# Scores of the first three head pairs as three fp32r products each, in a macaron transformer block on one core

## The reference, cut to what matters

```python
x = x + 0.5 * ffn(layernorm(x))        # gelu(h @ w1 + b1) @ w2 + b2, hidden 1024
q, k, v = heads(layernorm(x) @ w_qkv)  # 16 heads of 64
sim = (q * 64 ** -0.5) @ k.T + slope[h] * -abs(i - j)
attn = softmax(where(j > i, -max, sim))
x = x + (attn @ v) @ w_out + b_out
x = x + 0.5 * ffn(layernorm(x))
```

## Time and profile before

| what | value |
|---|---|
| median of 3 runs (lowest, highest) | 2183.58 us (2183.23, 2184.14) |
| the profiled execution's own time | 2183.17 us |
| its span, first to last instruction | 2181.4 us |
| mean granted TensorE clock | 0.995 |
| busy: PE, PEld | 98%, 80% of the span |
| busy: DVE, ACT, POOL | 69%, 57%, 48% |

### The profile page before, as it was taken

One profiled execution on the slowest core, in us unless ns is written; L12 is line 12 of the kernel. 1 busy time (PEld: TensorE's weight loads), 2 busy tenths in 40 slices (PEclk: granted clock), 3 DMA queues, 4 the chain that ended last, 5 costly groups with the idle time before them and its releaser, 6 DMA issues.

```text
span 2181.4 us, 41803 instructions
## 1 busy us (share of the span) xinstructions
PE 2137.8 (98%) x14720; PEld 1738.8 (80%) x14720; DVE 1507.9 (69%) x4014; ACT 1237.4 (57%) x3096; POOL 1056.4 (48%) x1770
## 2 busy tenths in 40 slices
PE   7999999999999999999999999999999999999997
PEld 6688787877878788787887878878787787878876
DVE  6866767667676676776768676676766767667674
ACT  5745646466464664736557364574646646466472
POOL 1744627446273553726537174372744627355371
PEclk9999999999999999999999999999999999999999
DMA  3422505234051331514315052250523405134151
GB/s 131 131 74 73 141 1 159 56 88 126 15 151 49 108 107 34 152 28 118 96 56 137 22 140 74 70 143 2 156 58 91 123 15 151 49 108 107 35 137 43
DMA packets 109985, 193.91 MB, mean 89 GB/s; under 512 B 34512, under 2 KB 53200, under 8 KB 109776
## 3 DMA queue, kind: packets, MB, share of 16 engines
q1 hardware_dynamic: 88816, 137.95, 22.3%
q0 software_dynamic: 20480, 52.47, 9.7%
q10 hardware_dynamic: 480, 0.82, 0.1%
HBM read 14.95 MB, written 8.39 MB: 11 GB/s over the span
## 4 chain that ended last, share of the span: by engine, by line
PE 87%; ACT 4%; POOL 4%; DVE 3%; issue 1%; SPq 1%; DMA 1%; DVEq 0%; ACTq 0%; POOLq 0%
PE ps L302 85%; POOL P L983 3%; ACT P L629 2%; PE ps L356 2%; ACT L629 1%; DVE P L821 1%; SPq L245 1%; ACT qk L589 0%; DVE x L768 0%; DMA PT<-P 0%; DVE gl L739 0%; DMA raw<-in_L_ffn_w 0%; POOL PT L245 0%; DVE gh L788 0%; ACT gt L607 0%
## 5 line engine op out<-in xcount | busy, mean ns | idle before, releaser
L983 POOL TENSOR_SCALAR P<-P,rs 128x512 f32<-128x512 f32 (+3 forms) x1024 | 540.7, 546 | 441.8 <-DVE rs L804 438.4
L629 ACT ACTIVATE P<-P,mx 128x512 f32<-128x512 f32 (+3 forms) x1024 | 564.1, 555 | 194.8 <-DVE mx L813 194.6
L245 POOL DMA_DIRECT2D PT<-P x640 | 322.7, 510 | 238.1 <-DVE P L821 216.3
L821 DVE STREAM_TRANSPOSE P<-P 128x1792 f32<-128x1792 f32 (+1 forms) x256 | 374.2, 1486 | 13.2 <-POOL P L983 12.7
L302 PE MATMUL ps<-PT,v 128*64 128x256 f32 (+1 forms) x3072 | 306.9, 349 | 8.5 <-DMA PT<-P 8.5
L302 PE MATMUL ps<-qk 64*128 64x512 f32 (+3 forms) x2048 | 311.0, 443 | 0.7 <-ACT qk L589 0.7
L302 PE MATMUL ps<-w2h,gh 128*128 128x256 f32 x1024 | 292.8, 286 | 0.6 <-DVE gl L739 0.4
L302 PE MATMUL ps<-w2l,gh 128*128 128x256 f32 x1024 | 289.7, 283 | 0.0
L302 PE MATMUL ps<-w2h,gl 128*128 128x256 f32 x1024 | 289.5, 283 | 0.0
L302 PEld LDWEIGHTS ps<-PT,v 128*64 128x64 f32 x3072 | 205.5, 137 | 104.6 <-issue 15.7
L589 ACT ACTIVATE qk<-ps 128x512 f32<-128x512 f32 x256 | 153.2, 598 | 228.0 <-PE ps L302 227.9
(11 more groups left out here) (83 smaller groups left out, 4403.7 us busy)
## 6 DMA issues: line engine op xcount, KB each, us to landing
PT<-P SPq DMA_DIRECT2D x1398, 80.0 KB, 2.6
PT<-P POOLq DMA_DIRECT2D x640, 80.0 KB, 2.7
x<-in_L_attn_x SPq DMA_DIRECT2D x16, 512.0 KB, 4.2
out_y<-x SPq DMA_DIRECT2D x15, 512.0 KB, 3.2
raw<-in_L_ffn_w SPq DMA_DIRECT2D x2, 512.0 KB, 5.8
raw<-in_L_ffn_w SPq DMA_DIRECT2D x1, 1024.0 KB, 8.8
rawq<-in_L_attn_w_qkv SPq DMA_DIRECT2D x1, 1024.0 KB, 6.8
rawk<-in_L_attn_w_qkv SPq DMA_DIRECT2D x1, 1024.0 KB, 8.8
```

The source lines that it names most:

```text
L245: e.dma_start(PT[c % 2][32 * m:32 * m + 32, g, :], P[c % 3][32 * g:32 * g + 32, m, :]).then_inc(landed.sem, 16)
L629: e.activation(p, p, ACT.Exp, bias=mx[:, r, i:i + 1], scale=-1.0, accum_out=sm[:, r, i:i + 1]).then_inc(s_ex.sem, 1)
L821: e.transpose(p, p).then_inc(s_tr.sem, 1)
L983: e.tensor_scalar(p, p, rs[:, 2 * (c % 2) + h, i:i + 1], 1.0, ALU.mult, ALU.mult).then_inc(s_nz.sem, 1)
```

## The change

It touches `scores` on TensorE, `proj_copy` on ACT, DVE's order, one wait of POOL, and the q and k buffers.

- Pairs c < NS = 3 of each batch (heads 0 to 5) are scored as three fp32r products: high with high, high with low, low with high, for each i, the two heads alternating inside each product. Pairs 3 to 7 stay in float32.
- For those pairs ACT, right behind the float32 copy of q, copies q and k together (128 x 1024) into `qkh` as fp32r, and DVE writes the low part over the float32 tile (`qkl` has the place of `qkf`). `scores` waits for that. ACT's copy waits for its own copy of q.
- DVE does this `qk_lo` for pair 1 behind the eight `gelu_split` and ahead of `add3(b - 1, 0)`; for pair 2 behind `add3(b - 1, 2)` and ahead of `inverse(b, 1, 1)`; for pair 0 of the next batch behind `normal(3, b, ...)` and ahead of `ln_lo(3, b, 0)`. POOL's `bias(3, b)` waits for the last of these.
- `add3(b - 1, 1)` moves ahead of the first half of `turned(b, 0)`.
- k is now stored in the order in which the scores read it, and `proj_copy` waits for the scores of the pair directly before; TensorE issues those scores ahead of the projection anyway.

```diff
+    NS = 3
+    qkh = place("qkh", [128, 2, T], F32R, QK)
+    qkf_at = [PP + 10240] + [QK + 4096] * (NS - 1) + [QK + 4096 * (c % 2) for c in range(NS, NC)]
+    qkf = [place(f"qkf{c}", [128, 2, T], F32, a) for c, a in enumerate(qkf_at)]
+    qkl = [place(f"qkl{c}", [128, 2, T], F32R, a) for c, a in enumerate(qkf_at[:NS])]
...
             def scores(b, c):
-                e.wait_ge(s_pc.sem, s_pc.at((b, ("q", c))))
+                if c < NS:
+                    e.wait_ge(s_kl.sem, s_kl.at((b, c)))
+                    parts = ((qkh, qkh), (qkh, qkl[c]), (qkl[c], qkh))
+                else:
+                    e.wait_ge(s_pc.sem, s_pc.at((b, ("q", c))))
+                    parts = ((qkf[c], qkf[c]),)
...
+                    for n, (q, k) in enumerate(parts):
+                        for h in range(2):
+                            hs = slice(64 * h, 64 * h + 64)
+                            keys = k[hs, 1, :].rearrange("p (m n) -> p m n", m=4)[:, :, 0:32 * (i + 1)]
+                            last = mm(score_block(h, i), q[hs, 0, i * 128:i * 128 + 128], keys,
+                                      n == 0, n == len(parts) - 1)
...
                 e.activation(dst, src, ACT.Copy).then_inc(s_pc.sem, 1)
+                if tile[0] == "q" and tile[1] < NS:
+                    e.wait_ge(s_pc.sem, s_pc.at((b, tile)))
+                    e.activation(qkh[:, :, :], qkf[tile[1]][:, :, :], ACT.Copy).then_inc(s_kh.sem, 1)
...
+            def qk_lo(b, c):
+                e.wait_ge(s_kh.sem, s_kh.at((b, c)))
+                residue(qkl[c][:, :, :], qkf[c][:, :, :], qkh[:, :, :]).then_inc(s_kl.sem, 1)
...
                     gelu_split(2, b - 1, range(NM))
+                qk_lo(b, 1)
+                if b > 0:
                     add3(b - 1, 0)
                 inverse(b, 0, 1)
                 biased(b, 1, 3)
                 biased(b, 1, 2)
                 inverse(b, 0, 0)
-                turned(b, 0, 1)
                 if b > 0:
                     add3(b - 1, 1)
+                turned(b, 0, 1)
                 turned(b, 0, 0)
                 biased(b, 1, 0)
                 biased(b, 1, 1)
                 if b > 0:
                     add3(b - 1, 2)
+                qk_lo(b, 2)
                 inverse(b, 1, 1)
...
+                if more:
+                    qk_lo(b + 1, 0)
                 ln_lo(3, b, 0)
...
                 power(3, b)
+                if b + 1 < NB:
+                    e.wait_ge(s_kl.sem, s_kl.at((b + 1, 0)))
                 bias(3, b)
```

More of the change, by code:

```diff
@@ L64, in build @@
     QK, V, PP, PT_AT, GT = R, R + 8192, R + 16384, R + 47104, R + 67584
-    qk = [place(f"qk{i}", [128, 2, T], F32, QK + 4096 * i) for i in range(2)]
+    NS = 3
[3 more added lines that the diff above has]
+    qkl = [place(f"qkl{c}", [128, 2, T], F32R, a) for c, a in enumerate(qkf_at[:NS])]
     v = [place(f"v{i}", [128, NT, 4, DH], F32, V + 4096 * i) for i in range(2)]
@@ L171, in build @@
     s_oa = Signal("out_copied", pairs)
+    split_pairs = [(b, c) for b, c in pairs if c < NS]
+    s_kh = Signal("qk_hi", split_pairs)
+    s_kl = Signal("qk_lo", split_pairs)
     s_lh = Signal("lh_done", units)
@@ L426, in scores @@
             def scores(b, c):
-                e.wait_ge(s_pc.sem, s_pc.at((b, ("q", c))))
+                if c < NS:
[4 more added lines that the diff above has]
+                    parts = ((qkf[c], qkf[c]),)
                 for i in QORDER:
-                    w = 128 * (i + 1)
                     for h in range(2):
@@ L433, in scores @@
                             held[h + {3: 0, 2: 2, 1: 4}[i]] = ("scores", b, c, 0 if i == 2 else i, h)
[L434 to L437, removed]
+                    for n, (q, k) in enumerate(parts):
[4 more added lines that the diff above has]
+                                      n == 0, n == len(parts) - 1)
+                            if n == len(parts) - 1:
+                                last.then_inc(s_qk.sem, 1)
             def values(b, c):
@@ L585, in proj_copy @@
                     n = pairs.index((b, c))
-                    if n >= 2:
-                        e.wait_ge(s_qk.sem, s_qk.at((*pairs[n - 2], QORDER[-1], 1)))
-                    dst = qk[c % 2][:, 0 if kind == "q" else 1, :]
+                    if n >= 1:
+                        e.wait_ge(s_qk.sem, s_qk.at((*pairs[n - 1], QORDER[-1], 1)))
+                    if kind == "q":
+                        dst = qkf[c][:, 0, :]
+                    else:
+                        dst = qkf[c][:, 1, :].rearrange("p (m j s) -> p j m s", m=4, s=32)
+                        src = src.rearrange("p (j m s) -> p j m s", m=4, s=32)
                 e.activation(dst, src, ACT.Copy).then_inc(s_pc.sem, 1)
+                if tile[0] == "q" and tile[1] < NS:
+                    e.wait_ge(s_pc.sem, s_pc.at((b, tile)))
+                    e.activation(qkh[:, :, :], qkf[tile[1]][:, :, :], ACT.Copy).then_inc(s_kh.sem, 1)
             def ln_hi(L, b, u):
@@ L936, in _ @@
             split_weight_lo("wv")
+            qk_lo(0, 0)
             e.wait_ge(s_id.sem, s_id.at("dist"))
```

## The result

The changed kernel takes 2186.48 us (median of 20 runs, 2183.18 to 2191.98), the kernel before 2183.61 us in its 20 (2179.61 to 2185.75). The ratio is 1.0016, 95% interval [1.0009, 1.0022]. I had forecast 2174.5 and a range of 2163 to 2185. Nothing is gained; 2.9 us are lost, and the median is above the range.

A forecast was written before the change was run, and what follows sets the result against it. TensorE's stream bounds the kernel, with one stall per batch; 0.79 us gained per batch b > 0, times 15 = 11.9, minus 2.9 for batch 0, leaves 9.0: 2174.5 us. Overall range 2163 to 2185, the main forecast's own 2168 to 2179.

The forecast's parts named there:

- Part 1: Scores' products on TensorE: a fp32r burst saves 0.27 us a pair, taking 0.11 us for a 128-column step.
- Part 2: Moved add on DVE: TensorE's stall at q 2, 0.58 us a batch, goes.
- Part 3, pair 1: Split chain (ACT copy, DVE residue) ahead of pair 1's scores: 0.25 us exposed, 15 times.
- Pair 2: Split chain ahead of pair 2's scores: residue ends near 332.8, scores due at 333.8, so covered.
- dear 128-column products: Rival in the scores: 128-column fp32r products cost as much as float32's, -0.05 a pair, 2184.8 us; 8%.
- exposed weight loads: Rival in the fp32r bursts: each of 12 steps pays 0.11 us for a weight load, 2232 us; 5%.
- heads in turn: Rival in the scores: the two heads run one after another in fp32r, 91 us more; 3%.
- Part 3, pair 0: Next batch's pair 0: chain covered, 0.9 us to spare; ln_hi and ln_lo slip 0.3 to 0.4, said to have room.
- Part 4: SP's queue: spread(b, 1) starts 0.55 to 0.6 us later, so a new wait of 0.35 us ahead of values(b, 1).
- Part 5: Batch 0, without feed-forward work to hide the split chain: +2.9 us, once.
- the chain through SP grows: Rival: SP's chain grows by more than the 0.7 us read and the gain is gone, 2183 to 2186 us; 9%.
- TensorE idle over 1 us in a step of b > 0: Named sign of a wrong forecast: PE idle over 1 us in any step of b > 0.

The follow-up runs named there:

- experiment 2: Kernel before with only the moved add, add3(b - 1, 1) ahead of both halves of turned(b, 0), all scores float32: 2177.94 us, 0.9971.
- experiment 8: Changed kernel without the moved add (add3(b - 1, 1) again between the halves of turned(b, 0)): 2206.29 us, 1.0099 to the kernel before.
- Experiment 3: Changed kernel with DVE doing qk_lo(b + 1, 0) behind ln_lo(3, b, 0) instead of ahead: 2195.79 us, 1.0055 to the kernel before.
- experiment 7: Changed kernel with load of x behind spread(b, 1), batch 0 float32, high copy and residue of pairs 0 and 1 in halves: 2165.19 us, 0.9911.
- experiment 9: Changed kernel with only the high copy and residue of pairs 0 and 1 in halves: 2177.57 us, 0.9975 to the kernel before.
- experiment 4: Changed kernel with batch 0's scores left in float32: 2181.89 us, 0.9993 to the kernel before.
- experiment 1: Changed kernel with SP's load of x for batch b + 1 behind spread(b, 1) instead of ahead: 2178.05 us, 0.9973 to the kernel before.
- experiment 5: Kernel before, all scores float32, with the moved add and the load of x behind spread(b, 1): 2173.75 us, 0.9952.
- experiment 6: Changed kernel with the load of x behind spread(b, 1) and batch 0's scores in float32: 2173.79 us, 0.9951 to the kernel before.

## Why the prediction was wrong

**Right, and in size.** Part 1: 0.25 us a pair against 0.27. The 128-column step, the least known price, is 0.11 as taken, but for a first one of 0.06. Part 2: the whole 0.58 us a batch, shown by experiments 2 and 8 from both sides. Part 3, pair 1: 0.24 against 0.25, with some luck: the rows give 317.74 + 2.33 = 320.07 against 319.91, 0.16 us. Pair 2 was covered. The rivals of dear 128-column products, exposed weight loads and heads in turn are out. By the rows, the second and third steps of 512 columns follow after 0.23 us with the load of the same rows inside, so no load is exposed there. By the sentence of the Trainium skill on row groups that I had weighed (TensorE: Matmul & The Clock Gate, Packing small matmuls, The mechanism), each of them would have been; this trace disagrees with it. The 0.11 of 128 columns agrees with the load cost on the same page (LDWEIGHTS), which puts 107 ns on 128 columns whatever the rows.

**Wrong 1: "`ln_hi` and `ln_lo` behind it slip by 0.3 to 0.4 and have more than that"** (Part 3, pair 0). I followed pair 0's chain up to the scores and gave its neighbours a room that I had not looked up. `ln_lo(3, b, 0)` frees the bank of the second `ln_transpose`, and its room was nothing: the slip comes out as 0.30 us, 15 times, 4.5 us. Experiment 3 shows that both engines carry it; experiments 7 and 9 take it away by shortening both.

**Wrong 2: "Its last DMA is issued at 346.9 and lands 2.2 us on"** (Part 4). The chain, its direction and its starting point were right, and the wait came where I said. Its size was 0.77, not 0.35. I carried the landing of the earlier trace rows over as a constant. In the mean over the batches the load of x was issued 1.2 us ahead of the spread, and it is 0.47 after; the last landing behind the last issue went from 2.07 to 2.89 us. The issues themselves did not get later against TensorE: from the scores of (b, 1) to the last one it is 27.01 us before and 26.85 after, because the 1.2 us held some play. In the one batch that I had read it is 0.54, so I saw none. In means the account closes for the profiled execution: the slack was 1.25; TensorE comes 2 x 0.25 + 0.58 = 1.08 earlier, the landing 0.82 - 0.16 = 0.66 later, which leaves 0.49 to wait; and where PE waits for a landing it starts 0.25 behind it. That is 0.74, against 0.77. These 0.25 us are a second term that my sum had at nothing. In experiments 3, 4 and 9, which leave SP's order as it is, the wait is 0.64, 0.56 and 0.61, so 0.77 is the high end. In the kernel before the load's own transfer was hidden; pushed against the spread that it delays, it is not. Experiment 1 moves the load alone, and the landing is 2.15 again.

How near the load stands is not all of it. In experiment 2 it also stands 0.47 us ahead and the last landing is 2.29, though there the eleven issues take longer; counted from the first issue to the last landing it is 9.66 us there and 9.88 in the changed kernel, against 8.99 before and 8.93 in experiment 1. And before, five batches have the load 0.51 to 0.74 ahead and still land in 2.05 to 2.15. POOL's five DMAs of the same spread are a rival: the first of them is issued 0.16 us behind the load in the changed kernel, 0.63 in experiment 2 and 1.75 before. No run moves them alone. Whether the 512 KB hold the same DMA engines or the memory behind them, no run tells either.

**Wrong 3: batch 0 "+2.9 us, once"** (Part 5). The exposed chains were about as forecast: 1.45 us ahead of scores(0, 0) and 2.35 more ahead of scores(0, 1). What the sum lacked is the clock: behind idle time of 3 us it can fall, and in the profiled execution that cost some 5 us, while the waits and bursts alone come to 2.4 without x3l, near the forecast 2.9. By experiment 4 batch 0 costs 4.6 us in the median; in the profiled execution its end comes 8.8 us later, 1.1 of them not from the change.

**The sum over the run.** In the two profiled executions it closes: 8.8 us up to the scores of (1, 0), -0.2 from there to those of (15, 0), +0.1 behind them, together the 8.8 us by which the spans differ. In the last part `values(15, 1)` has no wait, and the wait for PT ahead of `values(15, 6)` grows from 2.2 to 3.4 us, but the savings of this batch pay for it. For the medians it closes less well: quiet batches that bring nothing and 4.6 us for batch 0 would make 2188.2, and the median is 2186.5. No trace of a median execution of this kernel exists; that the quiet stretch differs by 1.7 us between this trace and experiment 4's, mostly in the waits ahead of `values(b, 1)`, is the likely place of the 1.7 us.

The rival "the chain through SP grows" gave 2183 to 2186 and had 9%. It held in part: of the forecast 11.9 us of the quiet batches 0.42 x 15 = 6 went there, and 4.5 into a wait that no rival had; batch 0 was dearer besides. My own range of 2168 to 2179 did not even hold its own terms: a wait of 0.8 us in place of 0.35, everything else as forecast, makes 15 x 0.34 - 2.9 = 2.2 us gained, 2181.4. And the sign of being wrong that I had named, TensorE idle over 1 us in a step of b > 0, came: 1.75 us ahead of `values(2, 1)`. The share of 0.73 for "faster" was too high for a gain of 9 us made of terms that each had a slack of under 1 us beside it.

**Does the change do anything?** The move is good by itself (0.9971). The fp32r scores save 0.25 us x 48 = 12 us on TensorE and give it all back as long as the split is one piece on each engine (experiments 5 and 6). Split in halves they bring 8.6 us.

## What to carry to other kernels

When a stream without holes gets shorter, look up the room of every neighbour of what you add, up to who waits for its bank or buffer; "has more than that" is a number to read. A landing time is not a constant: a large transfer issued just ahead of a series of small ones delays their last, and moving it behind them gave back 8.4 us here. Work that needs only half of its inputs (here the k part) should be split at that point and done when that half is there, and a first batch that has no other work to hide the split may keep the old form.

## What the runs showed of the hardware

- With a 512 KB load issued 0.47 us ahead of eleven 80 KB DMAs of SP, the last of them lands 2.9 us behind its issue in the mean, 3.8 at worst (2.3 in the mean in experiment 2, where POOL's five come later); with 1.2 us in the mean it is 2.1, and with the load behind them 2.15. The load itself took 5.7 us in b = 2.
- A TensorE instruction that waited for a DMA starts 0.25 us behind its landing, in every `values(b, 1)` of the changed kernel that had to wait.
- fp32r matmuls in half the rows, two heads beside each other, step by 0.23 us (512 columns), 0.17 (384), and 0.11 (128) where each has its own weights to load; the first of 128 columns, behind longer ones, takes 0.06.
- In batch 0 TensorE's granted clock falls to the 1.2 GHz level (0.54 to 0.61 in windows of 4 us) behind idle times of 3 us, not each time (experiment 1), and a `values` burst then takes 4.53 us, not 2.38. The waits of 0.1 to 1.8 us in later batches don't do this: from 100 to 2100 us the mean granted clock is 1.00.
- POOL's 128 x 1024 add takes 3.37 us, not 2.38, with 1.3 us of DVE's two-input subtractions beside it; DVE is not slowed. The Trainium skill (SBUF — State Buffer, SBUF: two separate sides) has GpSimd and a VectorE instruction with two SBUF inputs lock a shared port for whole instructions, the later one standing still; 0.97 us lost against 1.13 of overlap agrees with that, with POOL, which begins 0.16 us behind the first residue, as the one that stands. The second residue begins 0.44 us behind the add and is not held up either, which that sentence does not settle.
